# Second attention: weights rotated per position, q beside k in row halves, keys masked on leaving PSUM; its layer norm done tile by tile in the soft experts

## The chip, the cores and the metric

One core of a Trainium2 chip runs the whole program. The metric is the device time of one execution in microseconds. A core has a matmul engine (TensorE, "PE"), which loads a weight block ("PEld") and then streams columns past it, a vector engine (VectorE, "DVE"), an activation engine (ScalarE, "ACT"), GpSimd ("POOL"), and a queue processor for transfers (SyncE, "SP"). PE writes to PSUM, eight banks of 512 floats a lane; everything else lives in SBUF, 128 lanes wide.

## The reference, cut to what matters

64 images of 16 patches make 1,024 tokens of width 192. Two layers follow; the change is in the second attention and in the end of the first layer's soft experts.

```python
h = h + L0_ffn(layernorm(h))            # soft experts: 4 experts x 256 slots, 768 hidden
# second attention, per image of 16 tokens, 6 heads of 32, rank 48
x = layernorm(h)
q, k, v = x @ qA @ qB, x @ kA @ kB, x @ vA @ vB
q = q * cos + rot(q) * sin              # cos, sin depend on the token's position and on d
k = k * cos + rot(k) * sin
p = softmax(causal(q @ k.T / sqrt(32)))
h = h + (p @ v) @ o_w
h = h + L1_ffn(layernorm(h))            # routed experts, top 2 of 4 groups x top 2 of 8
```

The layer norm has no weights: `(x - mean) / sqrt(var + 1e-5)`. `x @ kA` has 48 columns; the position 0 to 15 of a token in its image sets the rotation.

## The kernel before

Tokens are held in 8 tiles of 128 (8 images each), as `g.h` (tokens down the lanes) and, after a layer norm, `g.xnT` (96 of the 192 features down the lanes, two halves). Stages run one after another, each a block with a barrier at its end; semaphores order the engines inside a block. All matmuls of the stages told of here are f32, and each shows as two MATMUL records (a transpose as one).

**Soft experts** (`slot_experts`). A loop over 64 images, written out. Per image: SP loads the image's hidden pieces (six transfers, `load_image`, into a ring of four buffers; those of images 0 and 1 were loaded in the stage before, that of image 4 takes the buffer of image 0 again); PE makes 6 hidden products (L1132), ACT puts a gelu on each (L1195), and PE mixes them over the slots (`mix`, L1149). GpSimd copies the image's 16 columns of combine weights into `cw` (L1117). Every second image DVE transposes the mixed sum out of PSUM (`leave`, L1210), PE multiplies it by `w2` a quarter tile at a time (`down`, L1158), and DVE gathers the product into `acc` (L1217). At a tile's end `finish` adds the four bias terms (L1224) and writes the tile of `g.h`. After the last image the last tile's whole `down` (24 blocks) and its gather and `finish` run alone.

**Second attention** (`attention1`). After a barrier and the clearing of the semaphores comes `layernorm` "ln2": 32 throw-away products on PE (`keep_busy`, L95), statistics, a root on ACT, the tiles normalized (L196), transposed on PE (L212) and copied to `g.xnT` by ACT (L225); its SP queue issues the weights, tables and masks. The next block computes: the low-rank products of q and k together and of v, in two halves of 512 tokens (L611, copied out at L668); then for q and k, two head groups and two halves, the product with `wb` and with its rotated copy `wr` (L620, N = 512), which DVE combines with the cos and sin tables (L714, L715, L717: 3 operations of 96x512 for each of 8 parts); values (L625, L672). K must be masked to one head at a time (`keys`, L598): for each unit of 128 tokens GpSimd makes one head of each group and DVE two, three units ahead in a ring. A unit then runs through `scores` (L265), the maximum (L313, L317), six exponentials (L289), the normalization of the probabilities (`L321`, `L731`), six transposes (L273), their way out through ACT (L297) and DVE (L304), `values` (L635), out through ACT (L678), `project` (L643) and the addition to `g.h` (L720). PE's order in unit u is scores(u+2), transposes(u), project(u-2), values(u-1). ACT splits the exponentials of unit u+1 in two halves, and waits for the transposes of unit u between them. The route and the routed experts follow.

## Time and profile before

| | |
|---|---|
| median of 3 runs | 1109.38 us (1108.49 to 1493.33) |
| the profiled execution | 1109.79 us, of which the span from first to last instruction is 1108.0 |
| PE busy | 987.2 us (89%), 7,464 matmul records |
| ACT busy | 661.1 us (60%) |
| DVE busy | 390.4 us (35%) |
| POOL busy | 275.5 us (25%) |
| granted TensorE clock, mean | 0.95 |

Busy time is the union of an engine's instructions. The granted clock is the share of full speed (2.4 GHz) that PE was given: 1.00 or 0.50 at any moment, so a value between them is a mix. Image loop: about 241 to 665 us. Second attention with its layer norm: 677 to 758.5 us. Routed experts: from 810 us.

### The profile page before, as it was taken

Reading aid. Unit: us, or ns where it says so; the run is one execution under the profiler, and the core shown is the slowest. Engines: PE = TensorE matmul, PEld = TensorE weight load, DVE = VectorE, ACT = ScalarE, POOL = GpSimd, SP = SyncE. Lnnn points to the kernel's source line nnn. Section 1 sums busy time; section 2 is a strip of 40 time slices with the busy share of each in tenths; the row PEclk is TensorE's granted clock in tenths of the full one; section 3 lists DMA queues with packets and bytes.
Section 4 is the critical chain, followed back from the end, with each engine's and each line's share of the span. In section 5 each row is a group of like instructions: output and inputs, shape, how many; then the busy total and the mean of one; then the engine's idle time right before and its main releaser. Section 6 shows DMA issues by size and latency. Waiting matters only on the chain. (4 is left out here: it accounts for less than half of the span.)

```text
span 1108.0 us, 20060 instructions
## 1 busy us (share of the span) xinstructions
PE 987.2 (89%) x7464; PEld 646.1 (58%) x7464; DVE 390.4 (35%) x1009; ACT 661.1 (60%) x1222; POOL 275.5 (25%) x279
## 2 busy tenths in 40 slices
PE   8869769779999999999999997885159999999997
PEld 8445435433444445444444445354149999999997
DVE  2666958550011111111111113765832222222233
ACT  0566848579888888888888881263114333344332
POOL 0111853230000000000000000100365556565541
PEclk9999879889999999999999999989569999999999
DMA  9000019989655555555555511004469999999985
GB/s 362 7 1 1 1 52 328 321 302 173 125 125 122 124 116 115 124 123 122 118 115 115 117 27 48 0 2 114 165 238 313 334 325 325 322 327 327 326 261 129
DMA packets 76140, 185.37 MB, mean 167 GB/s; under 512 B 15904, under 2 KB 34560, under 8 KB 75784
## 3 DMA queue, kind: packets, MB, share of 16 engines
q1 hardware_dynamic: 63804, 169.44, 51.8%
q0 software_dynamic: 11808, 14.39, 6.3%
q8 instruction: 60, 0.98, 0.4%
q14 instruction: 36, 0.29, 0.1%
q10 hardware_dynamic: 432, 0.26, 0.1%
HBM read 148.36 MB, written 35.69 MB: 166 GB/s over the span
## 5 line engine op out<-in xcount | busy, mean ns | idle before, releaser
L1195 ACT ACTIVATE sle_H<-sle_hp 128x1024 f32<-128x1024 f32 x384 | 367.3, 1024 | 53.7 <-PE sle_hp L1132 53.6
L1649 ACT ACTIVATE ext_H<-ext_hp,ext_bias 128x128 f32<-128x128 f32 x378 | 104.1, 398 | 161.3 <-issue 158.7
L1149 PE MATMUL sle_up<-sle_H,sle_cw 128*32 128x512 f32 (+1 forms) x2048 | 191.4, 492 | 0.0
L1210 DVE STREAM_TRANSPOSE sle_UT<-sle_up 128x256 f32<-128x256 f32 x64 | 37.3, 584 | 289.1 <-PE sle_up L1149 289.1
L1591 PE MATMUL ext_yp<-rmoe_w,ext_H 128*128 128x192 f32 x756 | 133.5, 326 | 1.1 <-issue 0.6
L1591 PEld LDWEIGHTS ext_yp<-rmoe_w,ext_H 128*128 128x128 f32 x756 | 121.5, 190 | 1.7 <-issue 1.7
L1747 POOL DMA_INDIRECT sum<-ext_y,ext_yi x61 | 97.1, 1592 | 92.0 <-DVE ext_gate L1671 48.7
L1117 POOL COPY sle_cw<-keep_CT 128x128 f32<-128x128 f32 x64 | 18.9, 296 | 388.0 <-PE sle_up L1149 387.9
L1132 PE MATMUL sle_hp<-keep_G,keep_dT 99*128 99x512 bf16 (+1 forms) x512 | 101.9, 332 | 8.0 <-PEq L913 6.8
L1149 PEld LDWEIGHTS sle_up<-sle_H,sle_cw 128*32 128x32 f32 x2048 | 53.5, 109 | 87.0 <-issue 73.4
L1132 PE MATMUL sle_hp<-sle_G,sle_dT 99*128 99x512 bf16 (+1 forms) x512 | 99.9, 327 | 1.3 <-ACT sle_H L1195 1.1
L1573 PE MATMUL ext_hp<-ext_xT,rmoe_w 128*128 128x128 f32 x756 | 96.0, 277 | 0.0
L1573 PEld LDWEIGHTS ext_hp<-ext_xT,rmoe_w 128*128 128x128 f32 x756 | 90.7, 194 | 0.0
L1132 PEld LDWEIGHTS sle_hp<-keep_G,keep_dT 99*128 99x128 bf16 x512 | 45.1, 99 | 76.8 <-ACT sle_H L1195 29.0
L1132 PEld LDWEIGHTS sle_hp<-sle_G,sle_dT 99*128 99x128 bf16 x512 | 44.4, 97 | 69.8 <-ACT sle_H L1195 30.3
L1738 POOL DMA_INDIRECT ext_x<-xn,ext_xi x63 | 62.1, 986 | 33.5 <-issue 27.2
L1158 PE MATMUL sle_up<-keep_w,sle_UT 128*128 128x192 f32 x384 | 67.3, 326 | 0.8 <-DVE sle_UT L1210 0.8
L1158 PEld LDWEIGHTS sle_up<-keep_w,sle_UT 128*128 128x128 f32 x384 | 61.7, 190 | 2.1 <-DVE sle_UT L1210 1.7
L1681 DVE COPY ext_yi<-rmoe_slot 128x1 uint32<-128x1 uint32 x63 | 9.7, 154 | 150.3 <-PE ext_yp L1591 150.3
L1015 ACT ACTIVATE hid_gp<-hid_gps 128x768 bf16<-128x768 f32 (+1 forms) x40 | 34.0, 850 | 35.1 <-PE hid_gps L1000 14.8
L995 PE MATMUL hid_gps<-pre_w,vit_xnT 128*128 128x384 f32 x128 | 47.5, 515 | 5.8 <-DVE hid_rest L1038 5.8
L1579 PE MATMUL ext_hp<-ext_xT,rmoe_w 64*128 64x128 f32 x756 | 51.5, 283 | 0.0
(272 smaller groups left out, 1177.9 us busy)
## 6 DMA issues: line engine op xcount, KB each, us to landing
rmoe_w<-W SPq DMA_DIRECT2D x126, 576.0 KB
pieces<-hid_gp SPq DMA_DIRECT2D x16, 1152.0 KB, 4.9
keep_G<-pieces SPq DMA_DIRECT2D x32, 288.0 KB, 4.1
sle_G<-pieces SPq DMA_DIRECT2D x32, 288.0 KB, 4.1
pieces<-hid_gp SPq DMA_DIRECT2D x8, 768.0 KB, 5.6
keep_G<-pieces SPq DMA_DIRECT2D x32, 192.0 KB, 4.2
sle_G<-pieces SPq DMA_DIRECT2D x32, 192.0 KB, 4.1
keep_CT<-xT SPq DMA_DIRECT2D x6, 512.0 KB, 6.0
```

What stands on the lines that cost most here:

```text
L995: pe.matmul(gps[(STEPS * i + e) % 4][:, half, 0:HALF], g.wideT[:, 0, tokens], g.w1[:, e - 1, half * HALF:(half + 1) * HALF], start=True, s ...
L1132: mm = pe.matmul(hp[k % DEEP][:, j, off:off + width], dT[b][:, c * P:(c + 1) * P], G[b][:, (c // 2) * HID + at:(c // 2) * HID + at + width ...
L1149: mm = pe.matmul(to[32 * e:32 * e + 32], cw[:, p, 2 * e + grp, :], H[:, p, h:h + width], start=(p == 0 and grp == 0), stop=(p == 1 and grp ...
L1158: mm = pe.matmul(yps, UT[:, par, b, :], g.w2[:, b, :], start=(b == blocks[0]), stop=(b == blocks[-1]))
L1195: act.activation(H[:, p, WIDTH * k:WIDTH * (k + 1)], hp[k % DEEP][:].rearrange("p a c -> p (a c)"), ACT.Gelu_apprx_tanh).then_inc(gelu_don ...
L1210: dve.transpose(UT[:, par, at // 32:(at + width) // 32, 32 * j:32 * j + 32], src.rearrange("p (b c) -> p b c", c=32)).then_inc(ut_done[ban ...
L1573: pe.matmul(hp[q][:, c % 2, (c // 2) * P:(c // 2 + 1) * P], rt.w1[:, w, c, :], xT[:, q, 0, :], start=(c < 2), stop=False)
L1579: mm = pe.matmul(hp[q][:, c % 2, (c // 2) * P:(c // 2 + 1) * P], rt.w1[rows, w, HC + c // 2, :], xT[rows, q, 1, :], start=False, stop=(c > ...
L1591: mm = pe.matmul(yp[:, 0:D], H[:, q, c, :], rt.w2[:, w, c, :], start=(c == 0), stop=(c == HC - 1))
L1649: act.activation(H[:, q, c, :], hp[q][:, c % 2, (c // 2) * P:(c // 2 + 1) * P], ACT.Gelu, bias=bias[:, q, c:c + 1]).then_inc(gelu_done, 1)
L1738: pool.indirect_dma_start(out=x[:, p, :], out_offset=None, in_=xn_dram, in_offset=bass.IndirectOffsetOnAxis(ap=xi[p][:], axis=0)).then_inc ...
L1747: pool.indirect_dma_start(out=sums[q], out_offset=bass.IndirectOffsetOnAxis(ap=yi[q][:], axis=0), in_=y[:, q, :], in_offset=None, compute_ ...
```

## The change

- A new class `Attention1` holds the second attention's weights from the start of the program. They and the cos and sin tables are loaded by SP in the soft experts, ahead of image 4's load; the tables lie in `g.xn` meanwhile. From image 8 to 23 GpSimd makes `turned`: the 16 rotated copies of `wb`, one for each position (`turn`, five operations a copy). The rotation is thus in the weights.
- The soft experts' DVE adds a tile's biases in its second pair (`add_bias`), gathers the last product straight into `g.h`, and normalizes tile after tile (`normalize`: a chain of 13 operations, the root by Newton steps on DVE). Tiles 0 to 5 are normalized inside the loop, tile 6 after the last `leave`, tile 7 after the last gather. On PE, `turn_rows` transposes tiles 0 to 6 between the last mix and the last `down`; after it come the low-rank products of the first 512 tokens and the transposes of tile 7. The memset of `cw` stands after a wait instead of ahead of it.
- `attention1` has no layer norm. It makes the low-rank products of the second 512 tokens, stores them by position, and multiplies in 4 steps (8 positions, one head group): per position one product for q on lanes 0 to 63 and one for k on lanes 64 to 127 (K = 64, 96 weight columns, N = 64). ACT copies q out, with a stride of 16 floats; k leaves PSUM three times, each times a head mask, on DVE in steps 0, 2 and 3 and on ACT in step 1. So keys of all units exist before the loop, and the loop has no `keys`. Values come from two lane halves in 8 products. ACT runs the six exponentials of unit u+1 together, ahead of unit u's copy.
- `rest` (stage "hid") and `probT` (first attention) lie in the memory of `turned`. Masks are loaded when `attention1` begins. ACT computes one exponential on 1 column first.

```diff
+class Attention1:
...
+        self.turned = kept.sb("at1_turned", [P, PATCHES, D])
...
+        flat = g.xn[:].rearrange("p i d -> p (i d)")
+        self.cos, self.sin = (flat[:, n * 512:(n + 1) * 512].rearrange("p (c d) -> p c d", d=32) for n in range(2))
...
+        self.loads = [(self.wb[:], a["qkB"]), (self.cos, a["cos_rows"]), (self.sin, a["sin_rows"]), (self.wa[:], a["qkA"]),
+                      (self.wva[:], a["vA"]), (self.wvb[:], a["vB"]), (self.ow[:], a["o_w"]), (self.hm[:], a["head_mask1"])]
...
+    def turn(self, pool, n):
+
+        heads = lambda x: x.rearrange("p (h r d) -> p h r d", r=2, d=16)
+        angle = lambda x, r: x[:, n, 16 * r:16 * r + 16].unsqueeze(1).to_broadcast([P, HEADS_U, 16])
+        own, other, dst = heads(self.wb[:]), heads(self.part[:]), heads(self.turned[:, n, :])
+        if n:
+            pool.wait_ge(self.turned_done, n)
+        for half in range(2):
+            pool.tensor_tensor(dst[:, :, half], own[:, :, half], angle(self.cos, half), ALU.mult).then_inc(self.step, 1)
+            pool.tensor_tensor(other[:, :, half], own[:, :, 1 - half], angle(self.sin, half), ALU.mult).then_inc(self.step, 1)
+        pool.wait_ge(self.step, 4 * n + 4)
+        pool.tensor_tensor(self.turned[:, n, :], self.turned[:, n, :], self.part[:], ALU.add).then_inc(self.turned_done, 1)
+
+    def to_low(self, pe, g, half, bank, ready):
+        for k in range(NKD):
+            mm = pe.matmul(bank[:], self.wa[:, k, :], g.xnT[:, k, half * 512:(half + 1) * 512], start=(k == 0), stop=(k == NKD - 1))
+        mm.then_inc(ready, 1)
...
+    def to_low_v(self, pe, g, half, bank, ready):
+        for k in range(NKD):
+            for c in range(2):
+                at = half * 512 + c * 256
...
+            w.to_low(pe, g, 1, sc[0][:, 0], low_ready)
+            w.to_low_v(pe, g, 1, sc[0][:, 1], low_ready)
+            pe.wait_ge(low_done, 2)
+            for n, (ph, grp) in enumerate(steps):
+                for c in range(8):
+                    for x in range(2):
+                        rows = slice(x * KQ, (x + 1) * KQ)
+                        mm = pe.matmul(qk[n][x][0:KD, c * IMAGES:(c + 1) * IMAGES], w.turned[rows, 8 * ph + c, grp * KD:(grp + 1) * KD],
+                                       w.low[rows, 8 * ph + c, :], start=True, stop=True)
                 mm.then_inc(qk_ready, 1)
-            for i in range(TILES):
-                pe.wait_ge(cs_done, 2 * (5 + i // 2))
-                pe.matmul(banks[i][:, 0:D], low_v[:, i * P:(i + 1) * P], wvb[:], start=True, stop=True).then_inc(v_ready, 1)
-
-            def operands(u, b):
-                return t.qT[:, b, u * P:(u + 1) * P], t.kTm[:, u % KEYS_DEEP, 3 * b:3 * b + 3, :]
+            pe.wait_ge(q_done, 2)
+            pe.wait_ge(k_dve, 1)
+            pe.wait_ge(k_act, 1)
+            for half in range(2):
+                for e in range(2):
+                    for c in range(2):
+                        rows, at = slice(c * KQ, (c + 1) * KQ), half * 256 + e * P
+                        mm = pe.matmul(vb[2 * half + c][:, e * D:(e + 1) * D], w.low_v[rows, at:at + P], w.wvb[rows, :], start=True, stop=True)
+                mm.then_inc(v_ready, 1)
...
+            for n, (ph, grp) in enumerate(steps):
+                act.wait_ge(qk_ready, n + 1)
+                act.activation(by_position(qT[0:KD, grp], ph), in_bank(qk[n][0]), ACT.Copy).then_inc(q_done, 1)
+                if n in ON_ACT:
+                    for dst, own in keys(n):
+                        op = act.activation(dst, in_bank(qk[n][1]), ACT.Copy, scale=own)
+                    op.then_inc(k_act, 1)
...
-            t.exps(act, 0, range(HEADS_U))
-            for u in range(UNITS):
+            exps(0)
+            for u in range(TILES):
...
-                if u + 1 < UNITS:
-                    t.exps(act, u + 1, range(HEADS_U // 2))
-                t.leave_act(act, u)
-                if u + 1 < UNITS:
-                    t.exps(act, u + 1, range(HEADS_U // 2, HEADS_U))
-            leave_values(UNITS - 2)
-            leave_values(UNITS - 1)
-
-        @block.gpsimd
-        def _(pool):
-            pool.wait_ge(rope_done, len(parts))
-            pool.wait_ge(w_in, 16 * len(loads))
-            for u in range(UNITS):
-                keys(pool, u, (0,), t.km_pool)
+                if u + 1 < TILES:
+                    exps(u + 1)
+                leave_transposed(u)
...
-            for x in range(2):
-                src = wb[:, x, :].rearrange("p (h r d) -> p h r d", h=HEADS_U, r=2)
-                dst = wr[:, x, :].rearrange("p (h r d) -> p h r d", h=HEADS_U, r=2)
-                dve.tensor_scalar(dst[:, :, 0, :], src[:, :, 1, :], -1.0, None, ALU.mult).then_inc(rot_ready, 1)
-                dve.tensor_copy(dst[:, :, 1, :], src[:, :, 0, :]).then_inc(rot_ready, 1)
-            for n, (x, grp, half) in enumerate(parts):
-                dst = (t.qT[0:KD] if x == 0 else t.kT[:])[:, grp, half * 512:(half + 1) * 512]
-                dve.wait_ge(qk_ready, n + 1)
-                if n >= 2:
-                    dve.wait_ge(rope_done, n - 1)
-                dve.tensor_tensor(rope[:, n % 2, 0, :], banks[2 * (n % 4)][0:KD, :], cosT[:], ALU.mult).then_inc(cs_done, 1)
-                dve.tensor_tensor(rope[:, n % 2, 1, :], banks[2 * (n % 4) + 1][0:KD, :], sinT[:], ALU.mult).then_inc(cs_done, 1)
-                dve.wait_ge(cs_done, 2 * n + 2)
-                dve.tensor_tensor(dst, rope[:, n % 2, 0, :], rope[:, n % 2, 1, :], ALU.add).then_inc(rope_done, 1)
...
+            for n in range(len(steps)):
+                if n not in ON_ACT:
+                    dve.wait_ge(qk_ready, n + 1)
+                    for dst, own in keys(n):
+                        op = dve.tensor_scalar(dst, in_bank(qk[n][1]), own, None, ALU.mult)
+                    op.then_inc(k_dve, 1)
...
+                if m == FIRST_TURN // 2:
+                    for dst, src in w.loads:
+                        sp.dma_start(dst, src).then_inc(w.w_in, 16)
...
+                if n == FIRST_TURN:
+                    pool.wait_ge(w.w_in, 16 * len(w.loads))
+                if FIRST_TURN <= n < FIRST_TURN + PATCHES:
+                    w.turn(pool, n - FIRST_TURN)
...
+            def turn_rows(i):
+                at = turns[i // 2 if i < TILES - 1 else -1]
+                pe.wait_ge(xn_ready, i + 1)
+                for k in range(NKD):
+                    to = (i % 2 * NKD + k) * P
+                    tr = pe.transpose(at[0:KD, to:to + P], g.xn[:, i, k * KD:(k + 1) * KD], g.ident[:])
+                tr.then_inc(xnT_ready, 1)
+
             for grp in range(2):
                 mix(IMAGES - 1, 1, grp, None, False, None)
+            for i in range(TILES - 1):
+                turn_rows(i)
             down((TILES - 1) % 2, IMAGES // 2, range(BLOCKS))
+            pe.wait_ge(xnT_done, NKD * 2)
+            w.to_low(pe, g, 0, hp[2][:, 1], low_ready)
+            w.to_low_v(pe, g, 0, hp[0][:, 0], low_ready)
+            turn_rows(TILES - 1)
...
+            for i in range(0, TILES - 2, 2):
+                leave_turned(i, 2)
+            leave_turned(TILES - 2, 1)
+            act.wait_ge(low_ready, 1)
+            w.leave_low(act, 0, hp[2][:, 1], low_done)
+            act.wait_ge(low_ready, 2)
+            w.leave_low_v(act, 0, hp[0][:, 0], low_done)
+            leave_turned(TILES - 1, 1)
...
-            dve.memset(cw[:], 0.0).then_inc(cw_zero, 1)
             for k in range(2):
                 dve.wait_ge(g.g_out[k], TILE_STORED * TILES // 2)
+            dve.memset(cw[:], 0.0).then_inc(cw_zero, 1)
...
+            def add_bias(t):
+
+                ht = g.h[:, t, :]
                 for e in range(SLOT_E):
-                    op = dve.scalar_tensor_tensor(acc[:] if e < SLOT_E - 1 else ht, b2[:, e, :],
-                                                  zn[:, bass.ds(t, 1), e:e + 1].rearrange("p o e -> p (o e)"),
-                                                  acc[:], ALU.mult, ALU.add)
-                    if e < SLOT_E - 1:
-                        c.after(op)
-                op.then_inc(h_done, 1)
+                    c.after(dve.scalar_tensor_tensor(ht, b2[:, e, :], zn[:, t, e:e + 1], ht, ALU.mult, ALU.add))
+
+            def normalize(t):
+
+                c.after(dve.bn_stats(stats[:], g.h[:, t, :]))
+                c.after(dve.bn_aggr(mv[:], stats[:]))
+                c.after(dve.tensor_scalar(ve[:], mv[:, 1:2], EPS, None, ALU.add))
+                c.after(dve.tensor_scalar(bits[:], ve[:].bitcast(U32), 1, None, ALU.logical_shift_right))
+                c.after(dve.tensor_scalar(r[:].bitcast(U32), bits[:], -1.0, ROOT_BITS, ALU.mult, ALU.add))
+                c.after(dve.tensor_scalar(ve[:], ve[:], -0.5, None, ALU.mult))
+                for _ in range(3):
+                    c.after(dve.scalar_tensor_tensor(sq[:], r[:], ve[:], r[:], ALU.mult, ALU.mult))
+                    c.after(dve.scalar_tensor_tensor(r[:], sq[:], 1.5, r[:], ALU.add, ALU.mult))
+                if t == 0:
+                    dve.wait_ge(w.turned_done, PATCHES)
+                dve.tensor_scalar(g.xn[:, t, 0:D], g.h[:, t, :], mv[:, 0:1], r[:], ALU.subtract, ALU.mult).then_inc(xn_ready, 1)
+                dve.wait_ge(xn_ready, t + 1)
...
+                    if tile:
+                        gather(tile - 1, j == 0, j == TILE_IMAGES // 2 - 1, pair - TILE_IMAGES // 2 + 1)
+                    if j == 1:
+                        add_bias(tile)
+                    if tile == 3 and j >= 2:
+                        normalize(j - 2)
+                    if tile >= 4 and j == 2:
+                        normalize(tile - 2)
...
+            normalize(TILES - 2)
+            gather(TILES - 1, True, True, (TILES - 1) * TILE_IMAGES // 2 + 1)
+            normalize(TILES - 1)
...
```

## Rows read from the trace of the kernel before

**Rows 1.** Times of each stretch from the last mix to the second attention's end.

```profile
665.46:677.40 11.94, 8.07 (x48) 7.77 (x48) 2.10 (x5) 0.00 (x0) 0.00 (x0) 1.00 0.00 0
677.40:687.12 9.72, 7.34 (x48) 6.82 (x48) 6.36 (x32) 3.78 (x10) 0.00 (x0) 0.82 0.50 135
687.12:694.30 7.18, 7.17 (x16) 2.24 (x16) 0.55 (x4) 1.78 (x3) 0.00 (x0) 1.00 0.00 0
694.30:713.05 18.75, 17.04 (x50) 7.71 (x49) 16.44 (x28) 3.87 (x10) 1.20 (x2) 1.00 0.00 0
713.05:717.18 4.13, 4.13 (x8) 2.23 (x8) 1.68 (x5) 0.62 (x1) 2.65 (x3) 0.59 0.00 0
717.18:758.51 41.33, 30.03 (x202) 20.01 (x200) 25.71 (x58) 23.93 (x112) 3.69 (x4) 0.88 0.01 1
```

**Rows 2.** Same view, a stretch of the soft experts' image loop.

```profile
300.00:400.00 100.00, 100.00 (x823) 47.43 (x823) 14.45 (x29) 86.10 (x91) 4.44 (x15) 1.00 0.54 118
```

**Rows 3.** Timeline of the soft experts' end (start, length, engine, line).

```profile
664.74 0.72 DVE L1210 STREAM_TRANSPOSE sle_UT<-sle_up 128x512 f32<-128x512 f32 x1 [0.41 <-PE sle_up L1149]
...
665.51 8.07 PE L1158 MATMUL sle_up<-keep_w,sle_UT 128*128 128x192 f32 x48 [0.84 <-DVE sle_UT L1210]
...
673.62 0.42 DVE L1217 SCALAR_TENSOR_TENSOR sle_acc<-sle_up,keep_rz,vit_h 128x192 f32<-128x192 f32 x1 [8.16 <-PE sle_up L1158]
...
677.44 0.88 DVE L181 BATCH_NORM_STATS2 ln_stats<-vit_h 128x6 f32<-128x192 f32 x3 [1.58 <-PEq L85]
```

**Rows 4.** Groups by line and form, 640 to 780 us (busy us, mean ns).

```profile
L196 DVE TENSOR_SCALAR vit_xn<-vit_h,ln_r,ln_nmr 128x192 f32<-128x192 f32 x16 | 4.8, 375 | 0.1
...
L181 DVE BATCH_NORM_STATS2 ln_stats<-vit_h 128x6 f32<-128x192 f32 x16 | 4.4, 347 | 2.1 <-PEq L85 1.6 <-PEq L571 0.5
...
L212 PE MATMUL at_sc<-vit_ident,vit_xn 128*96 128x128 f32 x16 | 2.1, 278 | 0.0
...
L225 ACT ACTIVATE vit_xnT<-at_sc 96x256 f32<-96x256 f32 x8 | 2.3, 396 | 2.7 <-PE at_sc L212 2.7
...
L194 DVE SCALAR_TENSOR_TENSOR ln_nmr<-ln_mv,ln_r 128x8 f32<-128x8 f32 x2 | 0.3, 167 | 0.1
```

**Rows 5.** Timeline: the first low-rank product leaves PSUM.

```profile
689.13 0.60 ACT L668 ACTIVATE at_low<-at_sc 112x512 f32<-112x512 f32 x1 [3.49 <-PE at_sc L611]
```

**Rows 6.** Timeline of the routed experts: whole rows, then row halves.

```profile
871.97 1.61 PE L1579 MATMUL ext_hp<-ext_xT,rmoe_w 64*128 64x128 f32 x24
...
873.78 1.50 PE L1573 MATMUL ext_hp<-ext_xT,rmoe_w 128*128 128x128 f32 x12
```

**Rows 7.** One line's instructions (ns min/median/max): keys leaving PSUM in attention one.

```profile
L513 DVE TENSOR_SCALAR pre_Dn<-at_b,at_bias,at_hm x12: 797/798/807, 33.2 to 51.5; 96x512 f32<-96x512 f32 x12
```

**Rows 8.** The same view: a strided write to SBUF.

```profile
L1712 DVE TENSOR_SCALAR ext_picks<-ext_kf x4: 223/234/464, 810.9 to 812.0; 128x63 f32<-128x63 f32 x4
```

**Rows 9.** Windows: one steady unit of the loop, and two microseconds earlier in it.

```profile
739.66:743.68 4.02, 3.41 (x27) 2.36 (x27) 2.88 (x7) 2.95 (x16) 0.00 (x0) 1.00 0.00 0
...
720.00:722.00 2.00, 2.00 (x5) 0.98 (x4) 0.61 (x1) 0.44 (x4) 0.00 (x0) 0.50 0.00 0
```

**Rows 10.** Timeline of that unit on PE, and the last unit's normalization.

```profile
739.66 1.53 PE L265 MATMUL at_sc<-at_kTm,at_qT 120*128 120x384 f32 x4 [0.61 <-ACT at_prob L289]
...
741.03 0.82 PE L273 MATMUL at_pt<-vit_ident,at_prob 128*128 128x128 f32 x6
...
751.63 0.96 DVE L731 TENSOR_TENSOR at_prob<-at_prob,at_rinv 128x768 f32<-128x768 f32 x1
```

**Rows 11.** Images 4's load and first use: timeline, and landing times of keep_G.

```profile
252.74 0.55 SPq L904 DMA_DIRECT2D keep_dT<-pieces  x1
...
265.19 0.60 PE L1132 MATMUL sle_hp<-keep_G,keep_dT 99*128 99x512 bf16 x3
...
DMA to landing us min/median/max: 4.2/6.3/7.3
```

**Rows 12.** One line's instructions: GpSimd adding 128 elements a lane.

```profile
L883 POOL TENSOR_TENSOR slw_part<-slw_part x8: 400/401/402, 107.8 to 143.8; 128x128 f32<-128x128 f32 x8
```

More of the change, by code:

```diff
@@ L658, in _, with keys @@
                     values(u - 1)
[L659 to L661 removed]
+            project(TILES - 2)
+            values(TILES - 1)
+            project(TILES - 1)
+        def keys(n):
+            ph, grp = steps[n]
+            return [(by_position(kTm[0:KD, 3 * grp + j], ph), w.hm[:, j:j + 1]) for j in range(GH)]
         @block.scalar
         def _(act):
[L665 to L668 removed]
@@ L1812, in build @@
                     with Scope(nc, "at0") as held:
[L1813 removed]
+                        first = Attention0(held, g, a, second.turned)
                         embed(nc, g, a["xT"], a["tokW"], a["pos_rows"], a["tok_b_rows"], first.loads, first.w_in)
```

388 lines of the change are left out of this document (186 added, 202 removed).

## The prediction

> **What bounds the kernel now.** I read the page's busy shares first (PE 89%, ACT 60%), then a windows table by stage, then the timeline of the stages that the diff touches. The image loop of the soft experts is bound by PE: in a stretch of 100 us PE is busy for all of it, ACT for 86 and DVE for 14 [rows 2]. So vector and GpSimd work can be put there, as long as nothing that PE waits for comes late. What lies behind the loop is different [rows 1]. From the last transpose of the mixed sum to the barrier is 11.94 us, of which PE works 8.07. The layer norm takes 9.72, the low-rank products 7.18, rotation and first keys 18.75 (PE 17.04, DVE 16.44: both nearly full), the first scores and maximum 4.13, the 8 units with their tail 41.33 (PE 30.03, DVE 25.71, ACT 23.93: nobody is full, so a chain of waits sets it). That is 93.05 us, from 665.46 to 758.51, and nothing of it is hidden. The sum below goes over these six stretches; route and routed experts are left as they are.
>
> **Stretches 1 and 2, the end of the soft experts and the layer norm (21.66 us before).** `turn_rows(6)` stands ahead of the last `down` on PE, and waits for `normalize(6)`, which DVE starts only after its last transpose. A `normalize` is a statistics operation (0.35), 11 small ones (0.17 each by the nearest row, an 8-wide one) and the final 192-wide one (0.375) [rows 4]; each waits for the one before, which costs some 0.04 more. Sum: 0.39 + 11 x 0.21 + 0.375 = 3.05 us. A transpose takes 2.1/16 = 0.13 [rows 4]. So `down` starts at 665.46 + 3.05 + 0.35 = 668.85 and not at 665.51 [rows 3]: a new stall of 3.3 us, behind which 48 records, DVE's last gather and the end are queued. `down` takes 8.07 as before, to 676.95; gather 0.45; `normalize(7)` 3.05; its two transposes and two copies of 128 columns 0.35 + 0.5 (256 columns take 0.40 [rows 4]): 681.35. In their cover lie the low-rank products of the first half: 3.6 us on PE (half of stretch 3, below) against 3.5 us that DVE needs for gather and norm; cover gone, they would cost themselves. The barrier with the clearing of semaphores was 675.86 to 677.44, 1.55 us [rows 3], and stays. The next block starts at 682.90: 17.44 us for 21.66. The removed `finish` operations (674.07 to 675.86) are in this.
>
> **Stretch 3, low-rank products (7.18 before).** Four products took 7.18, so two take 3.6 if the v product in column halves gains nothing, 2.8 if it gains all. The last copy out is half as long as one of 0.60 [rows 5], plus the lag of PSUM. I take 3.8: next at 686.7. The bounds are 3.1 and 4.1. The new exponential with its table load on ACT lies beside PE's first product.
>
> **Stretch 4, rotation and keys (18.75 before).** Gone are 16 products of N = 512 and 24 DVE operations. New are 4 steps of 16 products, 32 records each, K = 64, 96 columns of weights, N = 64. The nearest row is the routed experts' tail products, where lane halves take turns: 24 records in 1.54 us, 0.064 each, against 12 in about 1.34 (0.11) for whole rows [rows 6]. So halves do overlap. I take 0.064: 2.05 a step, 8.2 for four. Bounds: 0.05 (loads shorter by 96/128) and 0.11 (no overlap), so 6.4 to 14.1. Keys: three DVE operations a step in steps 0, 2, 3. Attention one's key operation, the same 96x512 out of PSUM, lasts 0.80 [rows 7], 0.7 from start to start, so 2.1 a step; DVE keeps up with PE and ends 2.1 after PE. ACT's four in step 1 and one in each other step fit in 8 us. Values and their copies fall beside the last keys.
>
> The new writes jump 64 bytes from element to element. The nearest row is a write that jumps 16 bytes: 63 elements in 0.23 [rows 8]; at one element a cycle, as the 0.375 for 192 against 0.167 for 8 suggests, about 0.23 is expected anyway, so no penalty shows. I put 0.8 us on the path for a small one, bounds 0 and 5 (every key operation twice as long). Together 8.2 + 0.3 (lag) + 2.1 + 0.8 = 11.4: next at 698.1. Range 9 to 20.
>
> The Trainium skill (SBUF — State Buffer, Door 1: The DMA port swizzle) says that each access that crosses into a new 16-byte line pays a penalty, so that only four floats a line run at full rate. By the row on the 16-byte jump, it does not show on DVE here; by the page these writes would be slower and the time that of rival C. Its page TensorE: Matmul & The Clock Gate (LDWEIGHTS) prices a load by its columns alone, P/1.2 ns: 80 ns for 96 columns, whatever the lanes. By that, 32 records take 2.56 us a step and the sum grows by 2; the tail products' row, 0.064 with 128 columns, disagrees.
>
> **Stretch 5 (4.13 before).** Scores were made at a granted clock of 0.59 [rows 1], and keys came late. At full clock the pair takes 1.57 and maximum with scaling 1.2: 2.8.
>
> **Stretch 6, the units (41.33 before).** A steady unit took 4.01 us, PE busy for 3.40, ACT 2.95, DVE 2.9 [rows 9]. Its chain: exponentials end, scores(u+2) for 1.4 [rows 10], transposes 0.8, ACT's copy 0.6, three more exponentials. With all six exponentials ahead of the copy this chain goes: ACT needs 3.1 a unit, PE 3.4, DVE 2.9 to 3.5 with its wait for scores. PE becomes the bound, about 3.5 a unit. Written out from the end of unit 0's exponentials, with starts as in the steady unit, the ends fall at 0, 2.1, 5.2, 8.6, 12.2, 15.7, 19.2, 22.8. Ahead of it lie unit 0's six (2.2), behind it the tail from the last normalization at 751.63 to 758.51 [rows 1, 10], 6.9 plus 0.3. Sum 32.2, at full clock. `keys` gone from GpSimd and DVE gives nothing beyond this.
>
> The clock: in the loop before it fell to 0.50 for some stretches, such as 720 to 722 [rows 9], after PE had waited for the exponentials; the stretch's mean is 0.88 [rows 1]. The new loop is denser on PE, but its start has the same wait, and PE now idles for 3 us ahead of `down` and 2 us at the barrier. I put 3.5 us on this, bounds 0 and 10.
>
> **Work put into the image loop.** GpSimd's `turn`: 16 times five operations of 96 or 192 elements, 0.35 to 0.55 each by the row of 128 elements (0.40) [rows 12], 2.2 us in an image of some 6; `cw` is copied first, so it costs nothing; if it blocks a DVE transpose, up to 0.3 us in each of 8 pairs, at most 2.5. DVE's norms: 3.05 + 0.45 us after a gather, ahead of a transpose due 8 us later: hidden. The eight loads (1.0 MB) take SP some 4 us, and are issued ahead of image 4's loads: those were issued from 252.74 on, within some 3 us, land 4.2 to 7.3 us later (by 263), and image 4 starts at 265.19 [rows 11]. Pushed by 3 to 4 us, they land at 266 or 267: a stall of 0 to 2 us that PE-bound work does not give back; I take 0.5. The memset after the wait delays GpSimd by 0.5, nothing behind it is that tight. Masks have 14 us until the first scores.
>
> **Sum.** 17.44 + 3.8 + 11.4 + 2.8 + 32.2 = 67.6 for 93.05: -25.4. Clock +3.5, load stall +0.5: -21.4. The profiled execution is 1109.8 (0.4 above the median), so 1088.4, at the median 1088. From page rules nothing enters.
>
> **Rivals.** A: nearly no clock loss and no stall, steps at 0.05: 67.6 - 2, so 1080 to 1085. For it speaks that the steady units before ran at 1.00. B: PE stays at the low clock through steps and first units, or halves of rows don't overlap (steps 14 us and not 8): +6 to +10 on the forecast, 1094 to 1098. For it: 0.59 and 0.88 above. Against: the measured 0.064. C: strided writes cost double: key operations 1.4 each, DVE 4.2 a step, last keys at about 5 us later, copies of q and low as well: 1093. D, slower than before: the same writes so slow that DVE's nine key operations outweigh everything. It decides at about 2.6 us more an operation (9 x 2.6 less 2 of slack = 21.4), 3.3 us for 512 elements; time 1110 or more. Nothing in the trace speaks for it but that no 64-byte jump is in it. E: the change's shorter chain does not show, since in the loop the cycle stays 4.0 because PE's order (transposes behind scores, values behind the copy) keeps the old chain: +3.5, 1092.
>
> **How the numbers follow.** Forecast 0.40 (1085 to 1091), A 0.21, B 0.14, C 0.10, E 0.12, D 0.03. Within 2% is about what a measurement of this kernel can tell from no change; the bound is 1087.2. All of A and half of the forecast's own share (1085 to 1091, of which the lower part is likelier) lie below it, 0.21 + 0.20 = 0.41, and 0.02 of C and E, where the clock is kind: 0.43. Slower by over 2% (above 1131) needs D and more: 0.02. Range 1080 to 1097, which leaves out D and the edges of A and B.
>
> **What would show it.** Right: `down` starts some 3.3 us later; the last block's first record at about 17.4 us after the last transpose; 32 records in about 2 us; DVE's key operations 0.7 to 0.9; units at 3.5 us with PE busy. Wrong: key operations above 1.2; a PE wait on a DMA at image 4; a granted clock under 0.8 between steps and unit 3; a layer-one loop longer than before.

## The result, and the profile after

The changed kernel took 1095.36 us (median of 4 runs, 1091.99 to 1098.95); the kernel before, on the same chip at the same time, 1112.23 (median of 4; one of them, a disturbed run of 1493.33, is left out of the ratio, and the other three took 1108.49, 1109.38 and 1115.08). The ratio is 0.986, 95% interval 0.981 to 0.990: a gain of some 16 us, 14.0 from the middle one of the three, and one that a bound of 2% calls "the same". The forecast of 1088 was 7.4 us too low.

The profiled execution took 1098.95 us, 1097.2 from first to last instruction (before: 1108.0). The windows view of the five stretches that are left, in the columns of [rows 1]: from the last transpose of the mixed sum to the next block's first product, low-rank products, rotation and keys, first scores, units.

```profile
674.38:692.24 17.86, 12.05 (x72) 9.74 (x69) 5.65 (x28) 3.89 (x13) 0.00 (x0) 1.00 0.00 1
692.24:697.44 5.20, 4.72 (x12) 1.53 (x13) 0.00 (x0) 2.88 (x4) 0.00 (x0) 0.59 0.61 143
697.44:711.16 13.72, 13.06 (x145) 12.70 (x145) 8.49 (x9) 8.17 (x11) 0.00 (x0) 0.53 0.02 5
711.16:713.92 2.76, 2.76 (x8) 1.40 (x8) 1.13 (x2) 0.26 (x1) 0.00 (x0) 1.00 0.00 0
713.92:746.29 32.37, 26.66 (x201) 18.29 (x200) 21.87 (x46) 23.83 (x112) 0.00 (x0) 0.95 0.00 1
```

Against [rows 1] the two first stretches together went from 21.66 to 17.86, the others from 7.18 to 5.20, 18.75 to 13.72, 4.13 to 2.76 and 41.33 to 32.37: 93.05 to 71.91 us, 21.1 less, where the prediction had 21.9 less with its clock term. The other parts of the span took some of it back:

| part | before | after | difference |
|---|---|---|---|
| start to the image loop's first product (same operations) | 241.06 | 245.06 | +4.0 |
| image loop | 424.40 | 429.32 | +4.9 |
| the five stretches | 93.05 | 71.91 | -21.1 |
| route and routed experts (unchanged) | 349.49 | 350.91 | +1.4 |
| span | 1108.0 | 1097.2 | -10.8 |

**The start** differs from execution to execution; the changed kernel and all its variants below have the same code there. The windows 40:80 us of the kernel before, of the changed one, and of the first experiment below show it, in this order; the granted clock is the third number from the end.

```profile
40.00:80.00 40.00, 28.92 (x386) 17.44 (x384) 25.09 (x55) 26.41 (x48) 4.20 (x8) 1.00 0.01 1
```

```profile
40.00:80.00 40.00, 30.39 (x359) 17.99 (x358) 24.16 (x51) 25.93 (x47) 3.54 (x6) 0.91 0.01 1
```

```profile
40.00:80.00 40.00, 32.66 (x332) 18.89 (x331) 23.71 (x49) 23.54 (x43) 2.51 (x5) 0.83 0.01 1
```

Clocks of 1.00, 0.91 and 0.83 there go with loop starts at 241.1, 245.1 and 249.3. In eleven profiled executions of changed kernels and one of before the start lies between 240.7 and 249.5: at a clock of 1.00 in that window between 240.7 and 241.3 (four executions), at 0.83 between 248.6 and 249.5 (five). The three between them are not in order (0.96 with 246.1, 0.87 with 244.3), so this window is not the whole of it. Less these 4.0 and 1.4 us, the two profiles differ by 16.2 us, which is close to the 16 of the ratio: this is the change.

**The image loop** is where a gain was lost. PE's timeline where image 4 begins (start, length, engine, line; in brackets the idle time ahead and who ended it). The hidden products in it are bf16, one record each, and not f32 like the other matmuls:

```profile
268.65 0.61 PE L1153 MATMUL sle_hp<-sle_G,sle_dT 99*128 99x256 bf16 x3
272.47 0.61 PE L1153 MATMUL sle_hp<-keep_G,keep_dT 99*128 99x512 bf16 x3 [3.21 <-DMA keep_G<-pieces]
273.00 2.51 PE L1170 MATMUL sle_up<-sle_H,sle_cw 128*32 128x256 f32 x16
275.44 2.11 PE L1153 MATMUL sle_hp<-keep_G,keep_dT 99*128 99x512 bf16 x8
277.48 1.50 PE L1170 MATMUL sle_up<-sle_H,sle_cw 128*32 128x256 f32 x16
278.91 1.47 PE L1153 MATMUL sle_hp<-keep_G,keep_dT 99*128 99x512 bf16 x8
```

PE waits 3.21 us for the transfer, and the two groups after the wait take 2.51 and 2.11 where the same groups take 1.50 and 1.47 four microseconds later: the clock in 272:277 was 0.66, against 1.00 on both sides. 3.21 + 1.01 + 0.64 = 4.86, nearly the whole of the loop's loss of 4.92. Before, image 4 started without a wait [rows 11]. The queue's timeline shows what stood ahead, and the view of `keep_G` how long image 4's last piece, issued at 264.21, then took:

```profile
256.71 0.42 SPq L1110 DMA_DIRECT2D keep_at_wb<-qkB  x1
...
260.01 0.43 SPq L1110 DMA_DIRECT2D keep_at_hm<-head_mask  x1
260.48 0.55 SPq L911 DMA_DIRECT2D keep_dT<-pieces  x1
261.07 0.58 SPq L913 DMA_DIRECT2D keep_G<-pieces  x1
...
DMA to landing us min/median/max: 8.2/8.2/8.2
```

Eight issues of 0.47 us shift image 4's by 3.8 us. Its last piece landed 8.2 us after its issue, at 272.4, and PE starts at 272.47; the same piece had taken 7.0 before. One issue of 1.26 us among those of image 4 adds some 0.7; before, the long issue fell behind them.

The lower clock does not follow each such wait. In a kernel of the experiments below (norm earlier), which has the same code up to here, the wait was shorter and the two groups behind it kept their length:

```profile
267.47 0.61 PE L1153 MATMUL sle_hp<-keep_G,keep_dT 99*128 99x512 bf16 x3 [2.46 <-DMA keep_G<-pieces]
268.01 1.50 PE L1170 MATMUL sle_up<-sle_H,sle_cw 128*32 128x256 f32 x16
```

In three of the seven kernels with the loads in this place PE waited 1.96, 2.35 and 2.46 us, the clock stayed at 1.00, and the loop was 2.1 to 2.4 us longer than before. In the other four it waited 2.62, 2.62, 3.08 and 3.21 us, the clock fell behind the wait, and the loop was 4.6 to 4.9 us longer. What made the waits differ was not looked for.

**The soft experts' end**, in the timeline, as predicted: a norm of 3.06 us, with `down` behind it.

```profile
673.66 0.72 DVE L1262 STREAM_TRANSPOSE sle_UT<-sle_up 128x512 f32<-128x512 f32 x1 [0.34 <-PE sle_up L1170]
674.30 0.32 DVE L1282 BATCH_NORM_STATS2 sle_stats<-vit_h 128x6 f32<-128x192 f32 x1
...
676.98 0.38 DVE L1293 TENSOR_SCALAR vit_xn<-vit_h,sle_mv,sle_r 128x192 f32<-128x192 f32 x1
677.41 0.42 PE L1209 MATMUL sle_hp<-vit_ident,vit_xn 128*96 128x128 f32 x2 [2.37 <-DVE vit_xn L1293]
677.67 7.97 PE L1179 MATMUL sle_up<-keep_w,sle_UT 128*128 128x192 f32 x48
```

**Rotation**, in the groups by line and form between 690 and 716 us (busy us, mean ns):

```profile
L705 DVE TENSOR_SCALAR keep_CT<-at_sc,keep_at_hm 96x512 f32<-96x512 f32 x6 | 5.6, 1065 | 2.2 <-PE at_sc L575 2.2
L575 PE MATMUL at_sc<-keep_CT,keep_at_turned 64*96 64x64 f32 x64 | 5.3, 364 | 0.0
L658 ACT ACTIVATE keep_CT<-at_av,keep_at_hm 96x512 f32<-96x512 f32 x3 | 2.8, 1081 | 0.0
L655 ACT ACTIVATE at_qT<-at_sc 96x512 f32<-96x512 f32 x2 | 2.1, 1066 | 0.6 <-PE at_sc L575 0.6
L517 ACT ACTIVATE keep_CT<-at_sc 128x512 f32<-128x512 f32 x1 | 1.0, 1049 | 1.4 <-PE at_sc L505 1.4
```

A key operation lasts 1.07 us where [rows 7] had 0.80 for the same form with neighbouring writes. 64 records of a step pair last 5.3, 2.56 a step from start to start where 2.05 was predicted. The windows view says at which clock: PE is busy throughout and gets half speed.

```profile
697.00:702.00 5.00, 4.56 (x58) 4.56 (x58) 1.68 (x2) 1.47 (x2) 0.00 (x0) 0.50 0.11 21
702.00:707.00 5.00, 5.00 (x68) 5.00 (x65) 2.80 (x4) 4.12 (x5) 0.00 (x0) 0.50 0.01 3
```

**Units** come every 3.36 us, and PE has no wait left in them (before: 4.01, with 0.61 of waiting for ACT [rows 9, 10]):

```profile
726.13 1.56 PE L593 MATMUL at_sc<-keep_CT,at_qT 120*128 120x384 f32 x4
727.52 0.82 PE L602 MATMUL at_pt<-vit_ident,at_prob 128*128 128x128 f32 x6
728.18 0.82 PE L619 MATMUL at_av<-keep_at_ow,at_oT 96*128 96x192 f32 x4
728.92 0.64 PE L612 MATMUL at_av<-at_probT,at_v 128*32 128x128 f32 x12
729.49 1.56 PE L593 MATMUL at_sc<-keep_CT,at_qT 120*128 120x384 f32 x4
```

### The profile page after: what moved, and what is told of

It is laid out like the page before. It is cut to its first block and busy times, and to the rows that moved or that the text cites. A ratio compares the mean times of both kernels' runs of the same rounds, so it can differ in the third digit from the quotient of the medians.

```text
span 1097.2 us, 20300 instructions
## 1 busy us (share of the span) xinstructions
PE 980.2 (89%) x7536; PEld 647.9 (59%) x7536; DVE 392.3 (36%) x1047; ACT 666.2 (61%) x1226; POOL 299.3 (27%) x351
```

## The experiments

All edits are made to the changed kernel. Because the start moves by up to 9 us between executions, single executions are compared stretch by stretch (in us, by their profiles): the loop, from its first product to the last transpose of the mixed sum; "end", from there to the next block's first product; then as above. Each experiment changes one or two columns; the others show how well a stretch repeats.

| kernel | loop | end | low | rotation | scores | units |
|---|---|---|---|---|---|---|
| changed kernel | 429.32 | 17.86 | 5.20 | 13.72 | 2.76 | 32.37 |
| loads later | 424.45 | 19.52 | 5.30 | 13.72 | 2.77 | 32.44 |
| norm earlier | 426.75 | 15.20 | 6.14 | 13.73 | 2.76 | 31.45 |
| neighbouring writes | 429.10 | 17.84 | 5.06 | 13.10 | 2.80 | 31.44 |
| exponentials split | 428.97 | 17.85 | 5.19 | 13.76 | 2.76 | 41.80 |
| 24 products ahead | 426.48 | 17.85 | 11.70 | 10.08 | 2.77 | 32.36 |
| halves apart | 426.76 | 19.53 | 6.14 | 19.75 | 2.77 | 32.37 |
| runs of 8 | 429.26 | 17.84 | 5.17 | 13.03 | 2.79 | 31.44 |
| loads and norm | 424.24 | 15.20 | 6.15 | 13.71 | 2.77 | 32.36 |
| these and copies | 424.41 | 15.20 | 6.14 | 12.84 | 2.79 | 32.37 |
| these and 8 products | 424.37 | 15.21 | 8.94 | 8.54 | 2.76 | 31.45 |

The units fall on 31.45 or 32.37 (once 32.44) without an edit to them: the clock in them is 1.00 or 0.95. "End" is 19.5 twice: the last `down` took 9.64 us there and not 7.97, its first four microseconds at a clock of 0.57. With the loads where the change put them PE waits for image 4 in all seven kernels, from 2.0 to 3.2 us, and the loop takes 426.5 to 429.3; with the loads moved it takes 424.2 to 424.5 in all four. A difference of 2.6 us between loops with the loads in the same place is thus no effect of an edit.

### Loads later

```diff
-        FIRST_TURN = TILE_IMAGES
+        FIRST_TURN, LOAD_AT = 12, 8
...
-                if m == FIRST_TURN // 2:
+                if m == LOAD_AT:
```

> The changed kernel with its eight loads issued ahead of image 8's and not image 4's, and the rotated copies made in images 12 to 27. Theory stall: the loads push image 4's data, so PE waits 3.2 us and then runs 1.7 us slower at the low clock; here PE has no wait on a transfer at image 4, and the image loop (first hidden product to last transpose) takes 424.4 us as in the kernel before, not 429.3: 5 us less time. Rival: the extra 1.0 MB takes transfer time wherever it is put, and a wait appears at image 8 or 9; loop still 428 to 430.

1096.54 us (median of 4; ratio to before 0.982, interval 0.975 to 0.988), not to be told from the changed kernel by its time alone. By its profile the loop is back at 424.45 us, before's 424.40, and PE has no wait of 3 us at image 4 any more. So the place of the eight loads in SP's queue cost the 4.9 us, and nothing else in the loop does: GpSimd's 34 us of `turn`, DVE's norms and the bias are hidden. Image 4's pieces landed at most 6.8 us after their issue here. Here the start was 249.3 and `down` lost 1.7 to the clock, which hid the gain in the total.

### Norm earlier

```diff
                     if tile >= 4 and j == 2:
                         normalize(tile - 2)
+                    if m == BODY - 1:
+                        normalize(TILES - 2)
...
-            normalize(TILES - 2)
             gather(TILES - 1, True)
```

> The changed kernel with normalize(6) moved from behind the last transpose to behind the last gather of image 63. Theory: PE's wait ahead of the last down goes, down starts right after its operands (some 0.4 us after the last transpose ends, behind 14 PE transposes) and not 3.3 us after it; the stretch from the last transpose to the next block's first product is 14.6 to 15 us for 17.86. Rival: DVE's norm now delays the last transpose, and the 3 us come back there: stretch short, but loop longer by 3 us.

The stretch falls by 2.66 us, to 15.20, and `down` starts 0.71 us after the last transpose instead of 3.29. So the wait for `normalize(6)` was real and avoidable. 0.9 of it comes back in the low-rank stretch, which then runs at a clock of 0.50 and not 0.59 (6.14 for 5.20). The two later kernels with this edit and no products ahead of the steps have 6.14 and 6.15 there as well. But halves apart has 6.14 without the edit, so that the edit causes it is likely and not shown.

### Writes to neighbours

All copies of q, k and low write 512 neighbouring floats. The values then lie in wrong places, with the same amount of work.

```diff
-        act.activation(self.low[:, :, half * 32:(half + 1) * 32].rearrange("p c b -> p b c"),
-                       bank.rearrange("p (b c) -> p b c", c=PATCHES), ACT.Copy).then_inc(done, 1)
+        act.activation(self.low.rearrange("p c b -> p (c b)")[:, half * 512:(half + 1) * 512], bank, ACT.Copy).then_inc(done, 1)
...
-            return x.rearrange("p (b c) -> p c b", c=PATCHES)[:, 8 * ph:8 * ph + 8, :]
+            return x[:, 512 * ph:512 * ph + 512].rearrange("p (c b) -> p c b", c=8)
```

> The changed kernel with the copies of q, k and low written side by side and not 16 (q, k) or 64 (low) floats apart; the values land in wrong places, so the attention's result is not the reference's, the work is the same. Theory stride: DVE's key operation goes from 1.04 us to 0.80 (0.7 from start to start), ACT's q copy from 1.06 to 0.69, the copy of low from 1.05 to 0.60; with steps still at 2.6 us the stretch from first step to first scores goes from 13.7 to about 12.7. Rival low clock: these engines do not follow TensorE's clock, but PSUM reads of 96x512 would be slow for another reason: durations stay above 1 us.

Groups by line and form of this kernel:

```profile
L704 DVE TENSOR_SCALAR keep_CT<-at_sc,keep_at_hm 96x512 f32<-96x512 f32 x6 | 4.1, 740 | 3.6 <-PE at_sc L574 3.6
L574 PE MATMUL at_sc<-keep_CT,keep_at_turned 64*96 64x64 f32 x64 | 5.3, 364 | 0.0
...
L654 ACT ACTIVATE at_qT<-at_sc 96x512 f32<-96x512 f32 x2 | 1.2, 592 | 2.2 <-PE at_sc L574 2.2
```

The stride is paid: 1.07 against 0.74 on DVE, 1.07 against 0.59 on ACT. But the stretch falls by only 0.6 us, where 1.0 was expected. PE's 5.3 us are unchanged, and DVE now waits 3.6 us for it where it waited 2.2: at half clock PE binds, and most of the copies' cost lies beside it.

### Exponentials split as before

```diff
                 if u + 1 < TILES:
-                    exps(u + 1)
+                    exps(u + 1, range(HEADS_U // 2))
                 leave_transposed(u)
+                if u + 1 < TILES:
+                    exps(u + 1, range(HEADS_U // 2, HEADS_U))
```

> The changed kernel with unit u+1's exponentials split again around unit u's copy, as before. Theory: ACT's order is what shortened the loop, so units go from 3.37 back to 4.0 us and the stretch from unit 0's first exponential to the end from 32.4 to 36 or 37. Rival: keys gone from DVE and GpSimd shortened it: units stay at 3.4 to 3.5.

The units take 41.80 us, as in the kernel before (41.33), though `keys` is gone from GpSimd and DVE. PE's timeline of this kernel:

```profile
735.84 1.56 PE L593 MATMUL at_sc<-keep_CT,at_qT 120*128 120x384 f32 x4 [0.52 <-ACT at_prob L673]
...
739.80 1.56 PE L593 MATMUL at_sc<-keep_CT,at_qT 120*128 120x384 f32 x4 [0.52 <-ACT at_prob L673]
```

The same PE instructions, 3.96 us a unit, with the wait for ACT back, as expected; the stretch is longer than the 36 or 37 us expected, and its clock is 0.84. The order of these exponentials on ACT is worth 9.4 us, the largest single gain that was taken apart: eight units times 0.6 are 4.8, the rest is clock and fill. How it splits between these two was not measured.

### Products ahead of the steps

```diff
+            keep_busy(pe, g, sc[1][:, 1], 24)
             pe.wait_ge(low_done, 2)
             for n, (ph, grp) in enumerate(steps):
```

> The changed kernel with 24 throw-away products of 128x128 (48 records) on PE ahead of the four steps; it costs 5 to 10 us itself. It tells what the steps are at full clock. In the changed kernel they ran at 0.50 for all of their 10.3 us, 0.080 us a record. Theory load: a record costs the load of its 96 weight columns, and that follows the clock: at 1.00 a record takes 0.04 to 0.05, a step 1.3 to 1.6 us. Theory fixed: the load costs 0.08 at either clock: steps stay at 2.56. Second question: whether the steps hold the clock; if small products do not count, the clock falls again inside them though PE has no gap.

PE's timeline of this kernel, and one row of its windows view:

```profile
698.99 6.61 PE L96 MATMUL at_sc<-vit_ident 128*128 128x128 f32 x48
705.53 1.57 PE L576 MATMUL at_pt<-keep_CT,keep_at_turned 64*96 64x64 f32 x32
706.94 1.53 PE L576 MATMUL at_av<-keep_CT,keep_at_turned 64*96 64x64 f32 x32
708.30 2.89 PE L576 MATMUL at_sc<-keep_CT,keep_at_turned 64*96 64x64 f32 x64
...
704.00:708.00 4.00, 4.00 (x73) 3.88 (x73) 0.84 (x1) 0.85 (x1) 0.00 (x0) 1.00 0.02 4
```

Entered at full clock, the same steps take 1.4 us each, 0.044 a record, and stay at 1.00. So what lies between these 1.4 and the 2.56 of the changed kernel is the clock. The products cost more than they bring here (6.5 for 3.6). Rotation ends 10.08 after its start, since DVE's nine key operations of 1.05 now bind.

### Halves apart

```diff
-                for c in range(8):
-                    for x in range(2):
+                for x in range(2):
+                    for c in range(8):
```

> The changed kernel with the 8 q products of a step first and then its 8 k products, so that lane halves do not take turns. Theory load: the price is one weight load after another whatever the half, a step stays at 2.56 us. Rival overlap: turns between halves hide half of each load behind the other half's product: a step takes 3.5 to 5 us, and the stretch from first step to first scores grows by 4 us or more from 13.7.

The starts of the steps in PE's timeline of this kernel (a step's bank is filled by q's half, then by k's; single records that the view shows between them are left out):

```profile
698.57 4.32 PE L575 MATMUL at_pt<-keep_CT,keep_at_turned 64*96 64x64 f32 x29 [0.48 <-ACT keep_CT L521]
702.53 0.42 PE L575 MATMUL at_av<-keep_CT,keep_at_turned 64*96 64x64 f32 x1
...
706.49 0.42 PE L575 MATMUL at_sc<-keep_CT,keep_at_turned 64*96 64x64 f32 x1
```

A step takes 3.96 us from start to start at the same half clock, 0.124 a record, where it took 2.56, 0.080 a record, with the lane halves taking turns. Rotation is 6.0 us longer. At half clock, halves in turn do overlap, by a factor of 1.5.

### Runs of eight

The copies walk image by image: eight neighbouring floats are written in SBUF, and the jumps, of 64 floats, lie in the read from PSUM.

```diff
-            return x.rearrange("p (b c) -> p c b", c=PATCHES)[:, 8 * ph:8 * ph + 8, :]
+            return x.rearrange("p (b c) -> p b c", c=PATCHES)[:, :, 8 * ph:8 * ph + 8]
...
-            return bank[0:KD, :].rearrange("p (c b) -> p c b", c=8)
+            return bank[0:KD, :].rearrange("p (c b) -> p b c", c=8)
```

> The changed kernel with the copies of q and k walking image by image, so that eight floats lie side by side in SBUF and the jumps are in the read of PSUM. Same result. Theory: the write's jump is what costs; DVE's key operation falls from 1.04 us to 0.8 to 0.9, ACT's from 1.06 to 0.7 to 0.8, rotation stretch 13.1 to 13.4 for 13.7. Rival: jumps in PSUM cost as much or more: operations at 1.04 or above, stretch 13.7 or longer.

Groups by line and form of this kernel:

```profile
L705 DVE TENSOR_SCALAR keep_CT<-at_sc,keep_at_hm 96x512 f32<-96x512 f32 x6 | 4.1, 740 | 3.6 <-PE at_sc L575 3.6
...
L655 ACT ACTIVATE at_qT<-at_sc 96x512 f32<-96x512 f32 x2 | 1.2, 592 | 2.2 <-PE at_sc L575 2.2
L517 ACT ACTIVATE keep_CT<-at_sc 128x512 f32<-128x512 f32 x1 | 1.0, 1039 | 1.4 <-PE at_sc L505 1.4
```

As fast as 512 neighbours, with every value in its place; only the copy of low, left as it was, still pays. It is the jump of the write that costs; the jump of the read, here of 256 bytes, costs nothing.

### Repairs together

First loads later and norm earlier together:

> The changed kernel with late loads and the early norm of tile 6 together. The two lie in different stretches, so they add up: loop 424.5 to 425 us for 429.3, end of the loop to next block 15.2 for 17.9; 7 us less than the changed kernel over these two. Time some 1088 to 1091, below both kernels; ratio to before about 0.979. Should they not add up, the norm's place delays the last transposes.

1095.36 us (median of 4; ratio 0.982, interval 0.974 to 0.990). Loop 424.24 and end 15.20: both gains add in the profile. The time does not show it: 1088 to 1091 was expected, and the median is that of the changed kernel. This profiled execution started at 248.7, the changed kernel's at 245.1, and the low-rank stretch took 0.95 more. Then the runs of eight as well, and low's copy walked so that it writes runs of 32 floats:

```diff
-        act.activation(self.low[:, :, half * 32:(half + 1) * 32].rearrange("p c b -> p b c"),
-                       bank.rearrange("p (b c) -> p b c", c=PATCHES), ACT.Copy)
+        act.activation(self.low[:, :, half * 32:(half + 1) * 32],
+                       bank.rearrange("p (b c) -> p c b", c=PATCHES), ACT.Copy)
```

> Three repairs together on the changed kernel: loads of the second attention issued later and image 4's first (FIRST_TURN 12, LOAD_AT 8), normalize(6) put right behind the gather of image 63, and the copies of q, k and low walked so that each write to SBUF runs over at least 8 neighbouring floats while the jumps lie in the PSUM read. Theory (three independent terms): against the version with the first two (69.3 to 70.2 us from the last transpose of the mixed sum to the end of attention) the copies give 0.7 us in rotation and up to 0.4 in the copy of low: 68.5 to 69.5 us, loop 424.3, so about 1092 where the loop starts at 249 and 1085 where it starts at 241; median some 8 us below the changed kernel's, ratio to the kernel before 0.980. The copy of low takes 0.60 and not 1.05. Rival (the stride of 64 bytes hurts a PSUM read as well once runs are 1 long): the copy of low stays at 1.05, and the time is that of the version with two repairs within 1 us.

1089.14 us (median of 6; ratio 0.980, interval 0.976 to 0.984). Rotation 12.84, the copy of low 0.60 for 1.05. Its read jumps 64 bytes and costs nothing. The low-rank stretch stays at 6.14, so the copy's 0.45 us do not show. Last, eight throw-away products (16 records) ahead of the steps:

> The kernel with the three repairs, plus 8 throw-away products of 128 columns (16 records) on PE between the low-rank products and the rotation's steps, where 24 were tried before. Theory 1 (what PE did just before the steps decides their clock, and little is enough): the ballast costs 2.2 us less the 0.5 that PE waits there anyway, the four steps fall from 10.6 to 5.6 us on PE, DVE's nine key copies of 0.74 then bind at about 8, so rotation from its first record goes from 13.0 to about 9: net gain 2 us or more. Theory 2 (8 are too few): clock stays at 0.50 in the steps, 64 records in 5.3 us, and the kernel is 1.7 us slower than the one without ballast.

The windows view of this kernel: the clock rises inside the eight products, and the steps get it.

```profile
691.00:694.00 3.00, 3.00 (x11) 0.99 (x10) 0.00 (x0) 0.70 (x2) 0.00 (x0) 0.50 0.60 132
694.00:697.00 3.00, 3.00 (x16) 3.00 (x16) 0.00 (x0) 0.28 (x1) 0.00 (x0) 0.55 0.00 0
697.00:700.00 3.00, 3.00 (x70) 2.88 (x69) 1.24 (x2) 0.59 (x1) 0.00 (x0) 1.00 0.00 0
```

The products cost 2.8 us, rotation falls by 4.3 to 8.54, and the first scores then wait for DVE's last key operation. By its profile the five stretches take 66.90 us instead of 69.34; 0.92 of this is the units at a clock of 1.00 for 0.95, which comes and goes without an edit, so 1.5 us are the products' net gain. By time, 1091.19 us (median of 6; ratio 0.979, interval 0.975 to 0.984) is not to be told from the kernel without them, nor either from a ratio of 0.98: the start's spread of 9 us is larger than what is looked for. Both lie below the changed kernel's ratio of 0.986, with intervals that overlap.

## Why the prediction was right and wrong

**The sum of the attention and what lies ahead of it came out right, by errors that cancel.** -21.1 us for the predicted -25.4 + 3.5 = -21.9. By its steps:

- `down` 3.3 us late: 3.29, behind a norm of 3.06 for 3.05. The two first stretches: 17.86 for 17.44; the barrier took 2.0 where 1.55 was put. Right.
- Low-rank products, 3.8: took 5.20. The mechanism of column halves is right (the v product lasts 1.08 us at full clock), but the granted clock in the stretch was 0.59. The clock's share was foreseen only as a lump. The copy of low, a strided write, lasts 1.05 for the 0.60 of [rows 5], which was not foreseen either; but ACT then waits 0.87 for the v product, and neither 0.45 us less (the repairs together) nor the neighbouring writes shortened the stretch beyond 0.14.
- Rotation, 11.4: took 13.72, inside its range of 9 to 20. The failed term is 0.064 a record: at full clock it is 0.044, below the lower bound of 0.05; at the half clock that it got, 0.080. The sum also left out the 2.6 us of values on PE as lying beside the keys; at half clock PE has 10.3 for the steps and 2.6 for values, together 12.9, and this is the 12.84 that is left when the copies are made fast. So rival B named the right cause (half clock through the steps), but its other condition, that row halves do not overlap, fell with the experiment of halves apart, and its first units ran at 0.95 and not at the low clock. The measured 1095.4 lies in B's band (1094 to 1098, chance 0.14) and outside the forecast's own (1085 to 1091).
- Strided writes: the penalty was put at 0.8 us on the path, and is 0.6 to 0.7. What was wrong is the reading that [rows 8] shows none: 63 elements are too few to see it (0.33 us on 512 elements would be 0.04 on 63, an estimate), and its jump is of 16 bytes and not 64. It is 0.33 us for each DVE operation and 0.47 for each of ACT's, so rival C's premise was half right (1.07, between 0.7 and its 1.4), and its price was not, since PE and not DVE bound the stretch.
- First scores, 2.8: 2.76. Units, 3.5 each and 32.2: 3.36 and 32.37. The experiment with the split turned exactly this chain back. Rival E (a cycle that stays at 4.0) fell, and D as well: no stretch but the loop became longer. A (1080 to 1085) had the right step time at full clock, but neither the clock nor the free loads that it assumed.
- Clock, +3.5: it cost about 6.4. Rotation lost 3.6 by the experiment with products ahead (10.08 at full clock), the units 0.9 (31.45 at 1.00), and the low-rank stretch some 1.8, an estimate: the first half's products, at full clock, with the copy behind them would make it 3.4. The terms themselves add up to 65.5 at full clock (17.86 + 3.4 + 10.08 + 2.76 + 31.45) where 67.6 was put. So the sum was 2.1 too high and the clock 2.9 too low; that only 0.8 is left is luck. The clock was lost in the steps and the low-rank products, and not, as was argued, mainly in the units' start.

**The load stall was wrong**, the step that made the forecast 4.4 us too low: 0.5 with bounds 0 and 2, measured 4.9. The shift of the issues was right (3 to 4 us; 3.8). It failed three times after that. First, 0.5 is less than its own rows give: loads that land at 266 or 267 for a start at 265.19 are a stall of 0.8 to 1.8. Second, the landing time was carried over from before (by 263), and image 4's last piece took 8.2 us where it had taken 7.0, and up to 6.8 with the eight loads moved; that the megabyte just issued lay ahead of it fits this, but no view shows it packet by packet. Third, the wait of PE was priced at its own length, while the clock fell behind it: another 1.65 us here, and nothing in the three kernels with a shorter wait. Moving the eight loads alone took the whole loss away. The sign by which this would be seen, "a PE wait on a DMA at image 4", was named in the prediction, and is what the trace shows.

**The rest of the miss.** The profiled execution was forecast at 1088.4 and took 1098.95, 10.6 more: 4.4 are the load stall, 0.8 the attention, and 5.4 the start and the routed experts, whose code the change leaves alone. The median is 3.6 below that execution, so of its 7.4 us of miss 5.2 are the two terms, if the median run has them as the profiled one has, and 2.2 are left. The base of 1109.4 is itself uncertain by as much: it is the middle one of the three runs above as well, but in the three later comparisons the same kernel took 1113.3, 1113.8 and 1111.3 (medians of 7, 7 and 11 runs). Whether the 2.2 come from the start's spread or from the base stays open.

**The two page rules that the prediction weighed.** The Trainium skill's page TensorE: Matmul & The Clock Gate (LDWEIGHTS), 80 ns for 96 columns and thus 2.56 us a step, gives the number that the changed kernel shows. This case's traces disagree with it as a rule all the same: 0.044 a record at full clock, 0.080 at half clock, and 0.124 at half clock with the halves apart, for the same 96 columns. The Trainium skill's page SBUF — State Buffer (Door 1: The DMA port swizzle) says that only so many floats as share a 16-byte line go at full rate. The direction agrees with the traces: 1.07 us for a write that enters a new line with each element, 0.74 for neighbours. The prediction had set this rule aside by a row that could not show it.

## What to carry to other kernels

A transfer put ahead of others in a queue delays them by its issue time (here 3.8 us for eight), and they may land later as well (8.2 us for 7.0). A wait on a PE-bound path can cost more than its length, when the clock falls behind it (here in four kernels of seven). Put such loads where the next transfer has slack (here four images later, worth 4.9 us). When a loop has nobody full, write out the order on the engine that stands in the middle: one reordering on ACT was worth 9.4 us here. Put the jumps of a rearranging copy in the PSUM read, and let the write run over neighbours (runs of eight floats were enough here; shorter ones were not tried).

## What the hardware showed that had not been expected

- Small products (64x64, K = 64) that follow one another without a gap stayed at a granted clock of 0.50 for all their 10 us when they were entered at it, and at 1.00 when they were entered at that. Sixteen records of 128x128 ahead of them made the difference: 2.56 us a step against 1.4. Which property of the small products leaves the clock low was not tried.
- With lane halves taking turns, 32 records take 1.4 us at full clock, 2.56 at half clock, and 3.96 at half clock when they are apart. At full clock the halves were not tried apart.
- A 96x512 copy out of PSUM with a write jump of 64 bytes costs 1.07 us on DVE and on ACT, for 0.74 and 0.59 without; with runs of 8 floats it costs nothing, and neither does a jump of 256 bytes in the PSUM read. A 128x512 copy on ACT costs 1.05 with a write jump of 256 bytes, 0.60 with runs of 32 floats and a read jump of 64 bytes.
- A wait of PE for a transfer was followed by a lower clock in the four kernels where it lasted 2.62 to 3.21 us, and not in the three where it lasted 1.96 to 2.46, in front of the same products.
- The same code before the image loop took 240.7 to 249.5 us, with granted clocks of 1.00 to 0.83 between 40 and 80 us. A change of less than 1% of this kernel is better judged by its stretches than by its total.
